# Six decay buffers, exponentials two slots ahead and no copy of A in a selective-scan kernel

## The reference

```
xn = rmsnorm(x) * norm_w;  xp, z = split(xn @ Win)
u = silu(causal_conv4(xp) + conv_b)
dt, B, C = split(u @ Wx);  delta = softplus(dt @ Wdt + bdt);  A = -exp(A_log)
h_t = exp(delta_t * A) * h_(t-1) + (delta_t * u_t) * B_t     (256 channels x 16 states)
y_t = sum over states of h_t * C_t, + u_t * Dp
x = x + (y * silu(z)) @ Wblk
```

## Time and profile before

| | us |
|---|---|
| median of 3 runs | 2012.53 (2012.32 to 2015.65) |
| the profiled execution, own time | 2010.69 |
| its span in the trace | 2009.1 |
| ScalarE busy | 1628.5 (81%) |
| VectorE busy | 1807.3 (90%) |
| TensorE busy, weight loads | 1811.3 (90%), 1139.7 (57%) |
| GpSimd busy | 1445.0 (72%) |

### The profile page before, as it was taken

How to read it: one execution, slowest core, us unless ns; L and a number is a source line. 1 busy time by engine, 2 the same in 40 slices (tenths; PEclk the granted TensorE clock), 3 DMA queues, 4 the chain that set the end, 5 groups by cost and what they waited for, 6 DMA issues and landing times. The chain is left out here.

```text
span 2009.1 us, 30384 instructions
## 1 busy us (share of the span) xinstructions
PE 1811.3 (90%) x10816; PEld 1139.7 (57%) x10816; DVE 1807.3 (90%) x1728; ACT 1628.5 (81%) x2957; POOL 1445.0 (72%) x1364
## 2 busy tenths in 40 slices
PE   6899999998988888998999999998986899999998
PEld 2444444444444444444444444444443699999997
DVE  3999999999999999999999999999999977777775
ACT  5999999999999999999999999999997434333332
POOL 2899999999999999999999999999999200000000
PEclk9999999999999999999999999999998999999999
DMA  8433333434343534433333333343435000000000
GB/s 266 95 77 95 77 95 78 109 84 101 88 106 80 115 81 94 95 77 95 77 95 77 95 78 96 85 107 78 107 65 155 1 12 12 12 11 12 6 4 9
DMA packets 79750, 155.88 MB, mean 78 GB/s; under 512 B 12016, under 2 KB 30064, under 8 KB 74992
## 3 DMA queue, kind: packets, MB, share of 16 engines
q1 hardware_dynamic: 73200, 135.52, 28.3%
q10 hardware_dynamic: 6400, 18.42, 3.0%
HBM read 128.86 MB, written 23.99 MB: 76 GB/s over the span
## 5 line engine op out<-in xcount | busy, mean ns | idle before, releaser
L801 DVE TENSOR_TENSOR_SCAN scan<-decay,dbu_ps 128x1024 f32<-128x1024 f32 x512 | 1146.3, 2268 | 64.5 <-issue 53.1
L463 POOL TENSOR_TENSOR scan<-scan,c_rep 128x1024 f32<-128x1024 f32 x255 | 692.7, 2716 | 104.1 <-DVE scan L801 104.1
L1026 PEld LDWEIGHTS dbu_ps<-ident,scan 128*128 128x128 f32 x4096 | 455.3, 141 | 437.6 <-DVE scan L801 208.0
L548 ACT ACTIVATE decay<-d_rep,a_cur 128x510 f32<-128x510 f32 x1024 | 664.7, 709 | 24.1 <-ACT dbc L572 12.0
L1026 PE MATMUL dbu_ps<-ident,scan 128*128 128x128 f32 x4096 | 552.0, 278 | 143.7 <-DVE scan L801 121.7
L457 POOL TENSOR_SCALAR scan<-du_t,b_t 128x256 f32<-128x256 f32 x896 | 561.6, 642 | 0.0
L616 ACT ACTIVATE scan<-du_t,b_t 128x256 f32<-128x256 f32 x1024 | 445.5, 494 | 2.6
L810 DVE TENSOR_TENSOR scan<-scan,c_rep 128x1024 f32<-128x1024 f32 x257 | 327.5, 1275 | 0.0
L740 ACT ACTIVATE decay<-dbu_ps 128x512 f32<-128x512 f32 x256 | 147.9, 597 | 203.2 <-PE dbu_ps L1225 182.8
L1011 PE MATMUL y_ps<-scan,sel 128*32 128x512 f32 x2048 | 274.7, 609 | 0.0
L1039 PE MATMUL pre_ps<-xn,w_pre 128*128 128x512 f32 x512 | 247.2, 606 | 5.0 <-DVE w_pre L790 5.0
(11 more groups left out here) (102 smaller groups left out, 1400.8 us busy)
## 6 DMA issues: line engine op xcount, KB each, us to landing
d_rep<-delta_rows SPq DMA_DIRECT2D x248, 256.0 KB, 5.9
c_rep<-c_rows SPq DMA_DIRECT2D x128, 256.0 KB, 4.5
delta_rows<-delta SPq DMA_DIRECT2D x62, 256.0 KB, 2.2
w_pre<-prepared_weights ACTq DMA_DIRECT2D x15, 866.0 KB, 4.4
prepared_weights<-scan SPq DMA_DIRECT2D x3, 1122.0 KB, 12.8
scan<-in_conv_w SPq DMA_DIRECT2D x4, 512.0 KB, 4.9
w_out<-prepared_weights SPq DMA_DIRECT2D x16, 128.0 KB, 2.1
sp_e<-in_x_rows SPq DMA_DIRECT2D x8, 256.0 KB, 3.5
```

Source lines behind the costliest of these rows:

```text
L463: nc.gpsimd.tensor_tensor(ring[slot % RING], ring[slot % RING], c_rep[par][:, slot // PRS, :].unsqueeze(1).broadcast_to([128, 2, TG]), ALU ...
L548: last = nc.scalar.activation(decay[slot % DEC][:, u, :, 1:], src[:, :, 1:], ACT.Exp, scale=a_cur[:, b, m:m + 1])
L801: nc.vector.tensor_tensor_scan(ring[slot % RING].rearrange("p u t -> p (u t)"), decay[slot % DEC].rearrange("p u a t -> p (u a t)"), dbu_p ...
L1026: last = nc.tensor.transpose(dbu_ps[slot % 2][:, u, 128 * j:128 * j + 128], dbu_t[m % 2][:, j, b, :, :].rearrange("p q c -> p (q c)"), ide ...
```

## The change

The decay buffers become six, numbered on through the steps, and `LEAD` is 2: in its slot ScalarE issues the exponentials for the slot two further on, and in slots 14 and 15 those of slots 0 and 1 of the next step. The wait for a free buffer takes the new count. The scale is read from `a_rep`, where the layer is known when the program is built, and `a_cur` with its copy and semaphore goes. Memory for the two new buffers comes from `sp_e`, `sp_w` and `a_cur`; the tiles that lived there move to `du_t`, `xn` and `sp_l`, and SyncE's first input loads wait for the last reader of `du_t`.

```diff
--- before.py
+++ after.py
@@ -30,7 +30,8 @@
 PRS = UNITS // 2
 SLOTS = M * PRS
 RING = 8
-DEC = 4
+DEC = 6
+LEAD = 2
 SZ = 3
 POOL_J = 2
 EPS = 1e-5
@@ -80,15 +81,12 @@
         xc_all = sb("xc", [128, 2, KT, TG])
         xc = [xc_all[:, i, :, :] for i in range(2)]
         dbc = sb("dbc", [NBC, TG])
-        sp_e = sb("sp_e", [128, KT, TG])
-        sp_w = sb("sp_w", [128, KT, TG])
         sp_l = sb("sp_l", [128, KT, TG])
         delta = sb("delta", [128, KT, TG])
         du = sp_l
         du_t = [sb(f"du_t{i}", [128, JT, DI]) for i in range(2)]
         b_t = [sb(f"b_t{i}", [128, JT, NS]) for i in range(2)]
         a_rep = sb("a_rep", [128, LAYERS, UNITS, M])
-        a_cur = sb("a_cur", [128, UNITS, M])
         ident = sb("ident", [128, 128])
         mean_w = sb("mean_w", [128, 128])
         sel = sb("sel", [128, CH])
@@ -162,9 +160,9 @@
         hid = [decay_all[:, 2 * i:2 * i + 2, :, :, :].rearrange("p i u a t -> p (i u) (a t)") for i in range(2)]
         y_hi = [y_parts[:, i, 0, :] for i in range(2)]
         y_lo = [y_parts[:, i, 1, :] for i in range(2)]
-        x_in = [sp_e[:, i, :] for i in range(2)]
-        x_fin = sp_w[:, 0, :]
-        res1 = sp_w[:, 1, :]
+        x_in = [du_t[0][:, 2 * i:2 * i + 2, :].rearrange("p j d -> p (j d)") for i in range(2)]
+        x_fin = xn[:, :, :].rearrange("p a t -> p (a t)")[:, 0:TG]
+        res1 = sp_l[:, 1, :]
         y_ff = [sz[:, 2, i, :] for i in range(2)]
         acc = [xc[0][:, i, :] for i in range(2)]
         stage = [delta[:, i, :] for i in range(2)]
@@ -223,7 +221,6 @@
         first_rep = sem("first_rep")
         first_loaded = sem("first_loaded")
         rep_ready = [[sem(f"rep_ready{i}_{p}") for p in range(2)] for i in range(2)]
-        a_cur_ready = sem("a_cur_ready")
         decay_ready = sem("decay_ready")
         scan_done = sem("scan_done")
         hc_dve = sem("hc_dve")
@@ -352,7 +349,7 @@
             def window(s, i, par):
                 nxt = 1 - par
                 if is_last(s):
-                    sp.wait_ge(delta_ready, STEPS)
+                    sp.wait_ge(dbu_ready, SLOTS * (STEPS - 1))
                     load_input(0, 0, 0)
                     load_input(1, 0, 1)
                 if has(s, 1) and not has(s, 0):
@@ -542,11 +539,13 @@
 
                     act.wait_ge(rep_ready[par][p // 2], Q * 16 * (i + par))
                 wait(act, scan_done, SLOTS * s + slot - DEC + 1)
+                if s == 0 and slot == 0:
+                    act.wait_ge(a_ready, 1)
                 for u in range(2):
                     b = 2 * p + u
                     src = d_rep[par][:, b, :].rearrange("p (a t) -> p a t", a=SPG)
-                    last = nc.scalar.activation(decay[slot % DEC][:, u, :, 1:], src[:, :, 1:], ACT.Exp,
-                                                scale=a_cur[:, b, m:m + 1])
+                    last = nc.scalar.activation(decay[(SLOTS * s + slot) % DEC][:, u, :, 1:], src[:, :, 1:], ACT.Exp,
+                                                scale=a_rep[:, s // GROUPS, b, m:m + 1])
                 last.then_inc(decay_ready, 1)
 
             def silus(s, par):
@@ -636,17 +635,11 @@
 
             def window(s, i, par):
                 nxt = 1 - par
-                if has(s, 0) and par == 0:
-                    wait(act, decay_ready, SLOTS * s)
-                    act.wait_ge(a_ready, 1)
-                    nc.scalar.activation(a_cur[:, :, :],
-                                         a_rep[:, bass.ds(i // (GROUPS // 2), 1), :, :]
-                                         .rearrange("p l b m -> p (l b) m"), ACT.Copy)\
-                        .then_inc(a_cur_ready, 1)
-                    act.wait_ge(a_cur_ready, i + 1)
                 for slot in range(SLOTS):
-                    if has(s, 0):
-                        exps(s, i, par, slot)
+                    if slot + LEAD < SLOTS and has(s, 0):
+                        exps(s, i, par, slot + LEAD)
+                    if slot + LEAD >= SLOTS and has(s, 1):
+                        exps(s + 1, i + par, nxt, slot + LEAD - SLOTS)
                     m, p = slot // PRS + 1, slot % PRS
                     if has(s, 0) and slot == 0:
                         outer(s, par, 0, FIRST[2], FIRST[3])
@@ -799,7 +792,7 @@
                 if slot % 2 == 0:
                     wait(dve, quad_done, SLOTS // 2 * s + (slot - RING) // 2 + 1)
                 nc.vector.tensor_tensor_scan(ring[slot % RING].rearrange("p u t -> p (u t)"),
-                                             decay[slot % DEC].rearrange("p u a t -> p (u a t)"),
+                                             decay[(SLOTS * s + slot) % DEC].rearrange("p u a t -> p (u a t)"),
                                              dbu_ps[slot % 2][:, :, :].rearrange("p u t -> p (u t)"), 0.0,
                                              ALU.mult, ALU.add).then_inc(scan_done, 1)
 
```

## The result

The changed kernel is **slower**: 2053.78 us (median of 4 runs, 2052.68 to 2057.8) against 2013.12 us for the kernel before on the same chip, a ratio of 1.0204 with a 95% interval of 1.0191 to 1.0218. The prediction was 2039 with a range of 2029 to 2053. The direction was right; the forecast was 15 us too low, and the measured time lies 0.8 us above the range.

What follows compares the result with a forecast made beforehand. ScalarE, full rather than held, was taken to bound the kernel. From 2010.7 us, +6.7 for the start, -11.5 for the hole and +31.2 for d_rep stalls gave 2037.1, so 2039 for the median, range 2029 to 2053.

Steps and rivals of the forecast that it cites:

- What bounds the kernel now: Opening analysis: ScalarE is full, busy 45.73 of a 47.64 us step, and waits for a free decay buffer only 10 times.
- The hole of slot 8: VectorE's late scan in slot 8, 1.77 us a step: closing it lets ScalarE's gate wait reach its floor, -11.5 us.
- A read in place: ScalarE in even steps: reading A without the copy takes out one activation, 0.21 us by its row, 0.24 by waits.
- Exponentials of the next step: ScalarE in slots 14 and 15: asking earlier for d_rep stalls it 2.0 us in even steps, +31.2 us in all.
- long lag: SyncE's d_rep loads 10.68 us after softplus in steps 4 and 6, not 8.99: two even steps cost 1.6 us more.
- I take no further cost: Work behind ScalarE's d_rep wait, on GpSimd and TensorE: coming 2.0 us later adds nothing; bound 1 us a pair of steps.
- The stall spreads: Rival: late du_t copies delay GpSimd's outer products and TensorE's transposes, another 1 us a pair of steps, 2051 us; chance 0.09.
- Step 30 at nothing: Last even step: its delay costs nothing, being used up about when the first scan of step 31 starts anyway.
- The start: Window 0: exponentials placed ahead of the last outer products delay the first gate activation from 56.75 to 63.4, +6.7 us.
- The sum: Total against the profiled execution: 2010.7 + 6.7 - 11.5 + 31.2 = 2037.1 us, so 2039 for the median.
- The rule cited in the prediction: A repeating gap on the engine to saturate can mean no room for the next tile; six buffers would give back 53 us.

## Why the prediction was wrong, and what in it held

**What bounds the kernel now: held.** ScalarE is full and hardly ever waits for a buffer. Where VectorE was given room, the pace became 47.24, by the working of "The hole of slot 8" 47.63 - 0.38 = 47.25. There 0.8 us more on VectorE cost nothing, and a copy of 0.21 us more on ScalarE did cost time. (30 x 0.38 is 11.4; the sum carries 11.5.)

**A read in place: held in kind.** The copy alone shows nothing (1.0007), and shows up where the wait is at its floor, with 0.12 a step and not 0.24.

**The hole of slot 8, -11.5: this step failed.** Its sentence "VectorE runs on through slot 8, gets up to 1.77 us ahead" is where it broke. VectorE ran on, met GpSimd's product, and got nothing ahead; the sign named for it, a wait for the transposes near slot 3, is missing in the even steps from 2 on. In place of 47.25, the 15 intervals from an odd to an even window took 47.67 in the mean, 0.42 too much, +6.3 us. That the collision is the cause is shown: with the product moved at either lead, and nothing else, they took 47.20. The prediction checked what VectorE would wait for, but not what would run on GpSimd at the time to which its instructions moved.

**Exponentials of the next step, +31.2: held,** as the sum of the 14 waits, 31.3. Moving w_out took them away. That the sum agrees to 0.1 is partly luck: thirteen waits were 2.15 in the mean where 2.0 was forecast, and one was long (3.28, step 10) where two were forecast; steps 4 and 6 had no long lag this time.

**"I take no further cost": failed.** The intervals from an even to an odd window, less their wait for `d_rep`, took 47.81 in the mean and not 47.25; over 14 that is +7.9 us. Nearly 5 of it is TensorE's clock. In steps 9, 17 and 19 TensorE idled some 2.4 us before the first transposes of the step, behind GpSimd's late outer products; the granted clock fell to half, and these intervals came to 51.5. Step 9 by busy times, the slow stretch and then the idle one before it, and TensorE:

```profile
489.60:494.20 4.60, 4.53 (x14) 2.69 (x15) 2.29 (x1) 4.60 (x11) 4.60 (x7) 0.63 0.00 0
486.00:489.60 3.60, 1.30 (x4) 0.23 (x2) 3.27 (x2) 3.60 (x8) 3.60 (x4) 1.00 0.00 0
```

```profile
489.67 1.57 PE L1019 MATMUL dbu_ps<-ident,scan 128*128 128x128 f32 x8 [2.38 <-POOL scan L454]
491.04 3.13 PE L1032 MATMUL pre_ps<-xn,w_pre 128*128 128x512 f32 x4
```

The place is the one named under "The stall spreads", but most of it is not a longer chain. Steps 3, 11, 15 and 23 idled as long and kept the clock; less their wait, their intervals are 47.5 to 47.6, against 47.35 where TensorE idled 1.4 us or less, and 49.2 where the clock fell. So late outer products cost 0.2 and a half-speed stretch another 1.6; the remaining 0.1 in each of the 14 is not traced.

**Step 30 at nothing: failed.** It waited 3.36 us, and the time from window 30 to the end grew from 523.75 to 527.4. With w_out moved, and so without that wait, it is 522.7: step 31 doesn't use the delay up.

**The start, +6.7: 5.3,** within its bounds of 4.5 and 7.9, with the first scan at 51.76 where 52 was named. That ScalarE's order is the cause is argued from the rows and not shown: with slot 0 in its old place the first scan came back, the time did not.

**The sum.** Forecast: +6.7 - 11.5 + 31.2 = 26.4. Measured: 5.27 + 2.76 + 31.27 + 3.65 = 42.95. Of the 16.5 missing, 14.2 are the two failed terms in the steps, 3.65 the end, and the start takes 1.4 back.

The Trainium skill, SBUF — State Buffer, section Who interferes with whom, says that VectorE and GpSimd share a pair of SBUF ports, that a VectorE instruction with two inputs in SBUF can't read beside a GpSimd instruction that reads SBUF, and that whichever began first makes the other wait. The trace agrees: the multiply, both inputs in SBUF, ends 1.08 us after a product that began before it, and the scan, with one input in PSUM, keeps 2.27 us beside the same product.

The rule cited in the prediction (Perfetto Trace Analysis, Optimization Strategy, of the Trainium skill) is not borne out here: the repeating gap went, and no time came back with it. By the rule it would have been 1964; 2053.78 was measured, and 2015.16 with one slot of lead, where hardly any new wait was added.

## What to carry to other kernels

A hole in an engine can be what keeps its instructions out of another engine's way, so before closing it, look at what the neighbour does in the time to which the work moves, and read "busy" by the mean duration of each group, not by its share. Work issued further ahead asks earlier for everything it reads, so follow each input back to the DMA queue that brings it and to what stands ahead of it there. Here one slot of lead, not two, and one product on GpSimd two short instructions later gave 0.5% less than before in place of 2% more; two slots gave 0.3% less once SyncE's load of w_out was out of the way.

## What the runs showed of the hardware

- VectorE's multiply and GpSimd's large products exclude each other for a whole instruction: 1.19 to 1.31 us alone or beside the product's last 0.2 us, 2.07 behind half a product, 3.17 behind a whole one, up to 4.6 behind two instructions. In each case it ends some 1.08 us after GpSimd's instruction does. It works the other way as well: GpSimd's multiply, 2.36 us, takes 3.25 to 3.35 where VectorE's began first. Behind GpSimd's short outer products the multiply lost only 0.1 to 0.2.
- At the start of odd steps TensorE's granted clock fell to half for 3.4 us after 2.36 to 2.47 us of idling in 3 of 7 steps of the changed kernel, and in none of the 7 that idled 1.25 to 1.40 us. What decides between equal idle times stays open.
- In the kernels with a lead TensorE also idles some 2.5 us about 26 us after the first gate activation, in nearly every step. There the clock fell in 12 of the steps 1 to 29 of the changed kernel and in 17 of those with one slot of lead, where the steps with the fall are no longer than those without, 47.65 us. So a half-speed stretch cost time at the one place and none at the other.
